# Two transformer layers on one core: when GpSimd asks for the rows of an expert's tile, and where VectorE makes the first tile's low parts

## The reference

```python
x = x + _L0_attn_ref(xn, ...) + _L0_ffn_ref(xn, ...)     # layer 0: attention and experts
xn = _layernorm(x, axis=-1)
x = x + _L1_attn_ref(xn, ...) + _L1_ffn_ref(xn, ...)     # layer 1
# in _L0_ffn_ref: 16 experts of 512 x 128, each token goes to 2 of them
def step(y, p):
    w1, b1, w2, b2, w3, b3, ge = p
    h = jax.nn.silu(xt @ w1 + b1) * (xt @ w2 + b2)
    return (y + ge[:, None] * (h @ w3 + b3), None)
z = jax.nn.silu(xt @ sw1 + sb1) * (xt @ sw2 + sb2) @ sw3 + sb3
return (y + z).reshape(shape)
```

## Time and profile before

| | us |
|---|---|
| median of 3 runs | 2642.59 |
| lowest and highest | 2640.86, 2643.15 |
| the profiled execution | 2645.89 |
| its span, first to last instruction | 2644.0 |
| TensorE busy | 2536.7 (96%) |
| GpSimd busy | 1359.3 (51%) |
| VectorE busy | 1118.6 (42%) |
| ScalarE busy | 1090.9 (41%) |

### The profile page before, as it was taken

How to read it: one execution, slowest core, us unless ns; L and a number is a source line. 1 busy time by engine, 2 the same in 40 slices (tenths; PEclk the granted TensorE clock), 3 DMA queues, 4 the chain that set the end, 5 groups by cost and what they waited for, 6 DMA issues and landing times.

```text
span 2644.0 us, 40129 instructions
## 1 busy us (share of the span) xinstructions
PE 2536.7 (96%) x13674; PEld 2181.6 (83%) x13674; DVE 1118.6 (42%) x1903; ACT 1090.9 (41%) x2031; POOL 1359.3 (51%) x1357
## 2 busy tenths in 40 slices
PE   7999999999999999879999999999999988969999
PEld 5788888888888888768888888888888877857777
DVE  6333333333333334763333333333333478864453
ACT  4443434444434443433434344344344347733332
POOL 5655555555555552765555555555555368831110
PEclk9999999999999999999999999999999999989999
DMA  4211111111111112211111111111111079821100
GB/s 152 94 46 53 46 46 46 61 46 46 52 54 46 46 46 70 99 47 54 46 53 46 46 46 61 46 46 52 54 46 46 21 253 322 273 92 48 33 32 32
DMA packets 73151, 187.81 MB, mean 71 GB/s; under 512 B 12098, under 2 KB 15826, under 8 KB 73094
## 3 DMA queue, kind: packets, MB, share of 16 engines
q1 hardware_dynamic: 64550, 170.26, 18.8%
q0 software_dynamic: 8544, 16.82, 2.3%
HBM read 168.13 MB, written 26.79 MB: 74 GB/s over the span
## 4 chain that ended last, share of the span: by engine, by line
PE 83%; DVE 7%; ACT 3%; DMA 3%; issue 2%; POOL 2%; ACTq 0%; POOLq 0%; SPq 0%; DVEq 0%
PE bank L88 23%; PE bank L89 23%; PE bank L90 23%; PE bank L931 4%; PE bank L917 4%; PE bank L933 2%; PE bank L918 2%; DMA exin<-xn_rows,ecur 2%; DVE el L1992 1%; ACT exth L1951 1%; ACT eh L1960 0%; ACT eh L1956 0%; DMA l_stage<-y_slots,slot_of 0%; POOL l_stage L2496 0%; DVE ebias L1991 0%
## 5 line engine op out<-in xcount | busy, mean ns | idle before, releaser
L88 PE MATMUL bank<-xh,wh 128*128 128x512 f32 x1400 | 558.9, 399 | 3.3 <-ACT bank L1132 1.8
L90 PE MATMUL bank<-xh,wl 128*128 128x512 f32 x1400 | 545.7, 390 | 0.0
L1603 POOL TENSOR_TENSOR wl<-raw,wh 128x512 fp32r<-128x512 f32 x196 | 251.2, 1297 | 165.8 <-ACT wh L1177 163.3
L1425 DVE TENSOR_TENSOR acc<-bank,acc 128x512 f32<-128x512 f32 x256 | 176.9, 691 | 339.7 <-PE bank L90 339.7
L89 PE MATMUL bank<-xl_sums,wh 128*128 128x512 f32 x800 | 315.5, 394 | 0.0
L88 PEld LDWEIGHTS bank<-xh,wh 128*128 128x128 f32 x1400 | 263.2, 188 | 56.9 <-ACT bank L1132 2.3
L90 PEld LDWEIGHTS bank<-xh,wl 128*128 128x128 f32 x1400 | 262.8, 188 | 56.9
L88 PE MATMUL bank<-wh,xh 128*128 128x256 f32 x1024 | 293.9, 287 | 4.1 <-DVE xl L476 3.4
L1388 DVE TENSOR_TENSOR ms<-bank,dcur 128x384 f32<-128x384 f32 x256 | 142.4, 557 | 354.9 <-PE bank L918 345.7
L90 PE MATMUL bank<-wh,xl 128*128 128x256 f32 x1024 | 291.4, 285 | 0.0
L89 PE MATMUL bank<-wl,xh 128*128 128x256 f32 x1024 | 291.2, 284 | 0.0
(11 more groups left out here) (335 smaller groups left out, 5326.3 us busy)
## 6 DMA issues: line engine op xcount, KB each, us to landing
raw<-in_w_pairs_dram SPq DMA_DIRECT2D x128, 512.0 KB, 3.9
raw<-in_o_pairs_dram SPq DMA_DIRECT2D x32, 512.0 KB, 3.1
eraw<-in_ex_dram SPq DMA_DIRECT2D x31, 513.0 KB
y_slots<-ey SPq DMA_DIRECT2D x31, 512.0 KB
dcur<-in_decay_dram SPq DMA_DIRECT2D x32, 384.0 KB, 2.9
eraw<-in_ex_dram SPq DMA_DIRECT2D x31, 256.0 KB
l_raw<-in_l_w_dram SPq DMA_DIRECT2D x28, 192.0 KB
out_dram<-acc SPq DMA_DIRECT2D x16, 256.0 KB, 2.1
```

Source lines behind the costliest of these rows:

```text
L88: pe.matmul(out, wh, mh, start=start and i == 0, stop=False, skip_group_check=True)
L90: ins = pe.matmul(out, wl, mh, start=False, stop=stop and i == n - 1, skip_group_check=True)
L1425: v.tensor_tensor(now[:, t, :], op[t % 2][:], now[:, t, :], ALU.add).then_inc(v_acc, 1)
L1603: pool.tensor_tensor(wl[:, cols], src, wh[:, cols].bitcast(F32), ALU.subtract).then_inc(w_lo, 1)
```

## The change

Five things are changed, all in the experts' stage.

1. VectorE's low parts of tile 0 are made in two pieces: those of the rows behind t = 4, and those of the weights w1 and w2 behind t = 6. Before, all of them stood behind t = 3.
2. GpSimd asks for the rows of tile 2 between its additions for t = 3 and t = 4. Before, it did so behind t = 7.
3. In each step GpSimd gathers tile i+4 before it makes the low part of w3 of tile i+1, not after it.
4. In each step the low part of a piece of layer 1's weights stands in front of the gather, and is that of piece i-1. Before, it stood behind the gather, and was that of piece i.
5. In each step SP stores y of tile i before it asks for piece i+2, not after it.

```diff
--- before.py
+++ after.py
@@ -1380,7 +1380,7 @@
                     split(UNITS, 1, i)
 
             def vector(v):
-                lead, rest = experts["vector"](v) if last else (None, None)
+                (lead_rows, lead_weights), rest = experts["vector"](v) if last else ((None, None), None)
                 def mask(u, i):
                     wait(v, pe_s, 8 * u + i + 1)
                     if i == 0:
@@ -1584,8 +1584,10 @@
                     finish(t)
                     if last:
                         add_old(t)
-                        if t == TPG - 1:
-                            lead()
+                        if t == TPG:
+                            lead_rows()
+                        if t == HTILES - 2:
+                            lead_weights()
                     elif t >= TPG:
                         add_x(t - TPG)
                 if last:
@@ -1735,9 +1737,11 @@
                 section_low(None, 2)
                 all_rounds(pool, run)
                 if last:
-                    lead, rest = experts["gpsimd"](pool)
+                    lead, second_rows, rest = experts["gpsimd"](pool)
                     lead()
                     for t in range(HTILES):
+                        if t == TPG:
+                            second_rows()
                         wait(pool, dma_x[t // TPG], 16 * TPG)
                         wait(pool, v_fin, t + 1)
                         pool.tensor_tensor(now[:, t, :], now[:, t, :], xbuf[t], ALU.add).then_inc(x_fin, 1)
@@ -1877,14 +1881,14 @@
             is_tile, i, _, n = tile(r, b, 3)
             if is_tile:
                 load3(i, n)
-            is_piece, i, _, n = tile(r, b, 2, PIECES)
-            if is_piece:
-                load_piece(i, n)
             is_tile, i, _, n = tile(r, b, 0)
             if is_tile:
                 sp.wait_ge(a_y, i + 1)
                 sp.wait_ge(v_y, i + 1)
                 sp.dma_start(y_tiles[i], yb[n][:]).then_inc(dma_y[n], 16)
+            is_piece, i, _, n = tile(r, b, 2, PIECES)
+            if is_piece:
+                load_piece(i, n)
 
         def rest():
             load12(1, 1)
@@ -1977,20 +1981,26 @@
         return lambda: run(-1, 0), lambda: all_steps(a, run)
 
     def vector(v):
+        def rows_low(i, n):
+            for h in range(2):
+                v.wait_ge(a_xh, i * 2 + h + 1)
+                v.tensor_tensor(xtl[n][:, 2 * h:2 * h + 2, :], xt[n][h][:], xth[n][:, 2 * h:2 * h + 2, :].bitcast(F32),
+                                ALU.subtract).then_inc(v_xl, 1)
+
+        def weights_low(i, n):
+            for j in range(2):
+                v.wait_ge(a_hi, i * 2 + j + 1)
+                if j == 0:
+                    wait(v, v_hf, i - 1)
+                    v.tensor_copy(bias[n][:], raw12[n][:, 2 * SEC:W12])
+                v.tensor_tensor(el[n][:, w(j)], raw12[n][:, w(j)], eh[n][:, w(j)].bitcast(F32),
+                                ALU.subtract).then_inc(v_lo, 1)
+
         def run(r, b):
             is_tile, i, half, n = tile(r, b, 2)
             if is_tile:
-                for h in range(2):
-                    v.wait_ge(a_xh, i * 2 + h + 1)
-                    v.tensor_tensor(xtl[n][:, 2 * h:2 * h + 2, :], xt[n][h][:], xth[n][:, 2 * h:2 * h + 2, :].bitcast(F32),
-                                    ALU.subtract).then_inc(v_xl, 1)
-                for j in range(2):
-                    v.wait_ge(a_hi, i * 2 + j + 1)
-                    if j == 0:
-                        wait(v, v_hf, i - 1)
-                        v.tensor_copy(bias[n][:], raw12[n][:, 2 * SEC:W12])
-                    v.tensor_tensor(el[n][:, w(j)], raw12[n][:, w(j)], eh[n][:, w(j)].bitcast(F32),
-                                    ALU.subtract).then_inc(v_lo, 1)
+                rows_low(i, n)
+                weights_low(i, n)
             is_tile, i, half, n = tile(r, b, 1)
             if is_tile:
                 v.wait_ge(a_s, i + 1)
@@ -2005,7 +2015,7 @@
                 wait(v, dma_y[n], half * 16)
                 v.tensor_copy(yb[n][:, 1, :], op[1][:]).then_inc(v_y, 1)
 
-        return lambda: run(-1, 0), lambda: all_steps(v, run)
+        return (lambda: rows_low(0, 0), lambda: weights_low(0, 0)), lambda: all_steps(v, run)
 
     def gpsimd(pool):
         def indices(i, n):
@@ -2035,24 +2045,20 @@
                 wait(pool, dma_x[n], half * 32)
                 indices(i, n)
                 pool.wait_ge(pe_xt, i * 2 - 2)
+            is_piece, k, _, nk = tile(r, b, -1, PIECES)
+            if is_piece:
+                c = bass.ds(k * PIECE, PIECE)
+                pool.wait_ge(a_l1, k + 1)
+                pool.tensor_tensor(w1l[:, c], l1raw[nk][:], w1h[:, c].bitcast(F32), ALU.subtract).then_inc(p_l1, 1)
+            if is_tile:
+                gather(n)
             is_3, i3, _, n3 = tile(r, b, 1)
             if is_3:
                 pool.wait_ge(a_hi3, i3 + 1)
                 pool.tensor_tensor(el[n3][:, w(2)], raw3[n3][:], eh[n3][:, w(2)].bitcast(F32),
                                    ALU.subtract).then_inc(p_lo3, 1)
-            if is_tile:
-                gather(n)
-            is_piece, k, _, nk = tile(r, b, 0, PIECES)
-            if is_piece:
-                c = bass.ds(k * PIECE, PIECE)
-                pool.wait_ge(a_l1, k + 1)
-                pool.tensor_tensor(w1l[:, c], l1raw[nk][:], w1h[:, c].bitcast(F32), ALU.subtract).then_inc(p_l1, 1)
-
-        def rest():
-            run(-1, 0)
-            all_steps(pool, run)
-
-        return lead, rest
+
+        return lead, lambda: run(-1, 0), lambda: all_steps(pool, run)
 
     return {"sync": sync, "tensor": tensor, "scalar": scalar, "vector": vector, "gpsimd": gpsimd,
             "stored": [(dma_y[b], 16 * ((NTILES + 1 - b) // 2)) for b in range(2)]}
```

## The result

| | before | after |
|---|---|---|
| median over 20 runs each, us | 2645.15 (2640.86 to 2650.11) | 2640.15 (2633.48 to 2642.95) |
| ratio, 95% interval | | 0.9977 (0.9969 to 0.9985) |
| profiled execution, us | 2645.89 | 2640.31 |
| its span, us | 2644.0 | 2638.5 |

The change makes the kernel 5.0 us faster, 0.23%, where 10.8 us were forecast. The direction was right, and the time lies above the range (2625 to 2639). A part of the distance is the base of the forecast: it was the median of 3 runs of the kernel before, 2642.59 us, and the median of 20 lies 2.6 us higher.

The account below looks back on a forecast made before the run. It saw the experts' stage bound by late gathered rows, nearly full DMA engines (0.97) and, in late steps, a VectorE-ScalarE ring. Terms -6.5 - 1.5 - 2.8 = -10.8 us took 2642.6 to 2631.8 us; range 2625 to 2639.

Parts of the forecast that it names:

- Term 1: Start of the experts' stage: tile 2's stall goes and tile 4's gather comes earlier, -6.5 us.
- Tile 2's weights: Start: w1 and w2 are requested later and ScalarE might wait, none to 5 us, eating most of Term 1.
- Term 2: Full steps: rows asked for ahead of w3's low part land earlier, -1.5 us (0 to -2.2).
- Term 3: The other, shorter steps: the bias copy no longer meets GpSimd's arithmetic, 0.2 us in 14 steps, -2.8 us (0 to -4).
- the ring: Late steps: VectorE and ScalarE, with the bias copy, set 5.56 us a step, falling by 0.75 to about 4.8.
- rival D: Steps: the lock between GpSimd and VectorE moves to a worse place, slower, about 2671 us; chance 0.07.
- rival A: Steps keep their pace and only Term 1 is real: 2636 us, or 2637 to 2639; chance 0.14.
- Edit 5 at nothing: Steps: storing y ahead of the piece's request is off the path and costs nothing.
- Rival C: Steps: what the start wins is paid back at full DMA engines, 2639 to 2643 us; chance 0.10.
- Rival B: Full steps fall to GpSimd's 5.35 us as the DMA engines gain too, needing 383 GB/s: 2624 us; chance 0.07.

Follow-up runs that it names:

- Experiment 3: The kernel after with both of VectorE's pieces of tile 0 behind t = 4; 2637.07 us, ratio 0.997 to the kernel before.
- experiment 9: The kernel after with w3's low part ahead of the gather again; 2644.9 us, ratio 0.9994 to the kernel before.
- experiment 8: The kernel after with GpSimd making only half of w3's low part from the third tile on, the rest left out; 2628.43 us, ratio 0.9934.
- experiment 10: The kernel after with y's store behind the request for the piece again; 2638.05 us, ratio 0.9974 to the kernel before.
- experiment 1: The kernel before with only VectorE's two pieces and tile 2's gather between the additions, old step order; 2645.3 us, ratio 0.9998.

## Why the prediction was partly right, and where it failed

- **What bounds the stage.** Right on late rows in the start and in the full steps. Wrong on the meaning of the DMA share: at 0.97 and 335 GB/s there was room for 359 to 362 GB/s in the same stretch of other kernels.
- **Term 1 (-6.5; tile 4 measured at -3.8 over two profiles each).** The mechanism of edit 2 was right: tile 2's gather starts 24.2 to 25.0 us behind the mark instead of 31.1 to 34.0, and TensorE no longer waits for it. The step that failed is that of edit 1: the piece behind t = 6 "delays `finish(7)` by at most 4 us, and that lies beside GpSimd's gather and additions, which end at 2142.6 either way; so I cost it at nothing beyond term 1". They didn't end either way. GpSimd's last addition needs `finish(7)`, and the additions locked the piece out until they had ended (its first copy for 4.32 us); what was left of it then cost GpSimd 2.03 us. Experiment 3 takes it away and finds the forecast start of the gather to 0.1 us. A second cause is the profile on which the sum was made: its start was 2.7 us longer than that of the second, with a granted clock of 0.72 in it. Tile 4's gather, from which the 6.5 us were taken, stood 44.7 us behind the mark there and 41.7 in the second profile; it was forecast at 38.2, experiment 3 has 38.3, and the kernel after 39.1 and 39.9.
- **Tile 2's weights** (the named danger to term 1) didn't hold ScalarE in the kernel after; the wait at 2146.03 is for VectorE's low part.
- **Term 2 (-1.5).** The direction of the mechanism was right, and experiment 9 shows that edit 3 carries it. Its size was wrong in two places: "2.3 us more for each landing" was 0.7, because GpSimd is not free when the transposes end, and the bound "6.12 x 0.97 = 5.94 us a step" was none: with the same loads, every step of experiment 8 takes less. The gain of the 25 steps, 4.6 us, lies entirely in those ahead of the late ones, which didn't change. That it comes near to terms 2 and 3 together (4.3) is luck.
- **Term 3 (-2.8).** Failed: late steps are 5.57 us as before. The step at fault is "With el moved behind the gather this copy meets no GpSimd arithmetic, and the ring falls by 0.75 [...] Next in line is GpSimd", at 5.35 us. The copy did become short, by 0.77 us. But `el` then met `ehl`, which grew by 1.22, and the ring fell by nothing. GpSimd's sum was wrong as it stood, too: its terms give 5.21, and with gaps of 0.2 to 0.3 this is 5.41 to 5.51, a gain of 0.05 to 0.15 us a step and not 0.2. Measured, `ecur` takes 0.40 for 0.19 (a lock), and 0.34 us of idle time stand behind it (experiment 9 has 0.35 to 0.39 there with an `ecur` of 0.20, so this is no lock), so that 0.40 + 0.34 + 1.02 + 0.15 + 1.04 + 0.30 + 1.01 + 1.30 is 5.56. That is rival D in a form that costs nothing net in a step, with A's result there.
- **The last step (+1.5)** was in no part of the prediction. The order of a loop's body was followed only where all its parts are present; at the end the gathers fall out and three long operations close up.
- **Edit 5 at nothing** held (experiment 10). **Rival C** holds for the start alone (experiment 1), not for the whole. **Rival B** named the right engine with too little room: GpSimd relieved gives full steps of 5.1 to 5.8 us at 359 GB/s, but its 383 GB/s was not needed, as few steps are full. Nor would it have been out of reach: just ahead of the stage, from 2124 to 2130 us, the DMA engines moved 403 GB/s in the kernel before, with other loads.
- **The rule of the Trainium skill** (SBUF — State Buffer, in the box of the section SBUF: two separate sides) that a float32 copy in SBUF keeps GpSimd from writing descriptors gave rival A a price of 0.17 us a gather. The trace doesn't bear it out as a cost here: with `ebias` beside the gather its first issue takes 1.04 us, and it took 1.39 in the old order. VectorE's low parts of the weights run beside it in both orders, so they alone don't explain the difference, which stays open. By the Trainium skill's section Who interferes with whom, on the same page, a lock lasts one instruction. In the first profile of before, the copy's 0.93 us end with one addition, which agrees; here the 4.32 us span three additions and the rest of a gather, and the measurement decides.

Sum: -3.8 - 4.6 + 1.5 = -6.9 in the profiles, -5.0 (0.15 to 0.31% of 2645) in the timed runs, against -10.8.

## What to carry to other kernels

When an operation is moved to where "the other engine is busy anyway", list what of the other engine waits for it, and check that the two don't lock each other out. The price of a lock isn't the length of the moved operation: plan with the other engine's unbroken row as the bad case (three operations in these traces) and with everything that the moved piece still has to do behind it. In the steps, taking the lock off one instruction put it on the next; shortening the engine that holds it moved the pace. A DMA share near 1 is a bound only when fewer bytes would shorten the step, and a run with a smaller load is the way to ask.

## What the runs showed that was not expected

- GpSimd instructions without a gap between them can keep VectorE out across several of them: 4.32 us for a copy of 128x2 beside the rest of a gather's issue and three additions (3.39 beside three additions), 3.81 us for a 128x256 subtraction over three operations. It isn't always so: that subtraction ended ahead of a fourth operation, and in the kernel before the copy got through behind one addition, or in 0.25 us at GpSimd's cost.
- It works the other way too: GpSimd's 128x2 copy, 0.17 to 0.19 us alone, takes 0.40 us behind VectorE's `ehl` and 0.73 behind its `el` pair, and four additions took 5.99 us instead of 5.04.
- A DMA share of 0.95 to 0.98 went with 321, 335, 344, 359 and 362 GB/s, in the same stretch of kernels with the same loads: the GB/s followed the pace of the steps, the share hardly moved.
- The same code ahead of the stage ended between 2108.45 and 2114.93 us, and a granted clock of 0.72 over 6 us of one execution went with a start that was 2.7 us longer than in the second profile.
